# Broadcast comparisons and scalings on VectorE, rewritten column by column, in a kernel of four graph layers

## The reference

```python
# layer L0, messages both ways along each edge
mi  = concat([x[src_bi], x[tgt_bi], ef_bi])
h   = relu(layernorm(mi @ msg_w1 + msg_b1)) @ msg_w2 + msg_b2
agg = segment_sum(h, tgt_bi)
# layer L1, softmax over the edges that leave a node
p   = exp(e - segment_max(e, src)[src])
p   = p / segment_sum(p, src)[src]
agg = segment_sum(normalize(feat)[src] * p[:, None], dst)
```

## Time and profile before

| | |
|---|---|
| median of 3 runs | 5807.9 us (5806.9 to 5809.72) |
| the profiled execution | 5813.95 us, its span 5812.2 us |
| VectorE busy | 4147.4 us (71%) |
| GpSimd busy | 4255.6 us (73%) |
| TensorE, ScalarE busy | 4197.8 us (72%), 3623.6 us (62%) |

### The profile page before, as it was taken

One profiled execution on the slowest core, in us unless ns is written; L12 is line 12 of the kernel. 1 busy time (PEld: TensorE's weight loads), 2 busy tenths in 40 slices (PEclk: granted clock), 3 DMA queues, 4 the chain that ended last, 5 costly groups with the idle time before them and its releaser, 6 DMA issues.

```text
span 5812.2 us, 83096 instructions
## 1 busy us (share of the span) xinstructions
PE 4197.8 (72%) x23224; PEld 3139.8 (54%) x23301; DVE 4147.4 (71%) x10603; ACT 3623.6 (62%) x12357; POOL 4255.6 (73%) x3819
## 2 busy tenths in 40 slices
PE   3766666666676666663688888568888884999995
PEld 2655565656565656663455555335555553555553
DVE  4867777777777676773688888657777775777775
ACT  3767666666667676762477777447767763555553
POOL 4788888888888888885477777577777753777776
PEclk6877777777777777776799999779999996999997
DMA  8776766666666767664366766456766662555553
GB/s 235 167 172 159 172 165 168 165 168 165 167 170 162 173 158 173 163 155 92 100 194 195 196 195 194 131 177 210 214 210 211 209 187 59 151 160 158 160 158 105
DMA packets 629375, 976.98 MB, mean 168 GB/s; under 512 B 105432, under 2 KB 339026, under 8 KB 628642
## 3 DMA queue, kind: packets, MB, share of 16 engines
q1 hardware_dynamic: 394242, 616.15, 33.6%
q0 software_dynamic: 234656, 355.35, 29.4%
HBM read 668.41 MB, written 306.11 MB: 168 GB/s over the span
## 4 chain that ended last, share of the span: by engine, by line
POOL 58%; issue 20%; PE 7%; DMA 6%; DVE 4%; ACT 2%; SPq 2%; POOLq 1%; DVEq 0%; ACTq 0%
POOL arena L1515 30%; POOL tab L1160 16%; POOL arena L1179 11%; DMA tab<-arena 3%; DMA arena<-T,srcI 2%; PE PS L1978 1%; POOLq L1173 1%; PE PS L1678 1%; POOL arena L1212 1%; PE PS L301 1%; PE PS L1956 1%; PE PS L1473 1%; ACT arena L1269 0%; SPq L786 0%; PE PS L1359 0%
## 5 line engine op out<-in xcount | busy, mean ns | idle before, releaser
L1515 POOL DMA_INDIRECT arena<-T,srcI x2112 | 2033.0, 963 | 843.9 <-issue 631.4
L1160 POOL DMA_INDIRECT tab<-arena x784 | 1286.9, 1641 | 279.4 <-issue 228.7
L1179 POOL DMA_INDIRECT arena<-T,srcI x784 | 802.4, 1023 | 286.5 <-issue 283.8
L1502 DVE TENSOR_TENSOR_SCAN arena<-arena,PS 128x512 f32<-128x512 bf16 x588 | 748.6, 1273 | 181.0 <-PE PS L2256 81.5
L851 PE MATMUL PS<-arena 128*128 128x128 f32 x1568 | 308.5, 358 | 674.3 <-ACT arena L1107 674.3
L1482 ACT ACTIVATE arena<-PS 128x512 f32<-128x512 f32 x588 | 347.3, 591 | 646.0 <-PE PS L1473 646.0
L1582 DVE TENSOR_SCALAR arena<-PS,nodeid 128x512 bf16<-128x512 f32 x908 | 627.6, 739 | 75.4 <-PE PS L1563 75.4
L851 PEld LDWEIGHTS PS<-arena 128*128 128x128 f32 x1568 | 265.5, 256 | 713.5 <-ACT arena L1107 713.5
L932 DVE CUSTOM_DVE_ANT_0 arena<-arena,ltri 128x128 f32<-128x128 f32 x784 | 224.7, 287 | 499.2 <-ACT arena L1083 499.2
L832 PE MATMUL PS<-We,arena 65*128 65x256 f32 x1568 | 513.9, 411 | 86.3 <-DVE arena L874 60.5
L2238 PE MATMUL PS<-arena 128*128 128x512 bf16 x2323 | 546.5, 382 | 4.4 <-issue 0.4
(11 more groups left out here) (287 smaller groups left out, 10294.5 us busy)
## 6 DMA issues: line engine op xcount, KB each, us to landing
H<-arena SPq DMA_DIRECT2D x784, 256.0 KB, 2.3
arena<-keepR SPq DMA_DIRECT2D x294, 256.0 KB, 5.2
arena<-sF SPq DMA_DIRECT2D x98, 512.0 KB, 5.8
arena<-wF SPq DMA_DIRECT2D x98, 512.0 KB, 7.2
arena<-dF SPq DMA_DIRECT2D x98, 512.0 KB, 8.6
arena<-T,srcI POOLq DMA_INDIRECT x2896, 3.8
arena<-in_ea64T SPq DMA_DIRECT2D x98, 256.0 KB
arena<-S SPq DMA_DIRECT2D x98, 256.0 KB
```

What stands on the lines that cost most here:

```text
L1160: e.indirect_dma_start(out=tabs[k % KT], out_offset=at_rows(iA[b % 10][:, c:c + 1]), in_=X2[b % 3][:, c, :], in_offset=None, compute_op=AL ...
L1179: e.indirect_dma_start(out=Gs[b % NR][:, c, :], out_offset=None, in_=T0, in_offset=at_rows(srcI[:, CB * b + c:CB * b + c + 1])).then_inc(g ...
L1502: ins = e.tensor_tensor_scan(s[b % n][:, h, :], kR[g % 6][:, h0:h0 + CB * P], src[h], s[(b - 1) % n][:, h, CB * P - 1:CB * P] if b else in ...
L1515: e.indirect_dma_start(out=dst[:, c, :], out_offset=None, in_=T_tab, in_offset=at_rows(srcI[:, CB * b + c:CB * b + c + 1])).then_inc(gs.of ...
```

## The change

Each tensor_tensor with a broadcast column becomes a row of tensor_scalars, one to a column, whose scalar is a [128, 1] operand, so each has one streamed input in place of two. `OH` is gone: `RH` is now made in 16 instructions of 25 elements, each a comparison and a multiplication by two [128, 1] operands; for that the mask `fst` is first multiplied by `mg` and by `sg` (two instructions of 8 elements, into the new `first`).

```diff
             def dve_S1(e, b):
...
-                e.tensor_tensor(Sm[b % 6], sR[g % 3][:, h0:h0 + CB * P].rearrange("p (c f) -> p c f", f=P),
-                                bf(srcF[:, CB * b:CB * b + CB]), ALU.is_equal).then_inc(S1.of(0), 1)
+                for c in range(CB):
+                    k = CB * b + c
+                    ins = e.tensor_scalar(Sm[b % 6][:, c, :], sR[g % 3][:, h0 + c * P:h0 + (c + 1) * P], srcF[:, k:k + 1],
+                                          None, ALU.is_equal)
+                ins.then_inc(S1.of(0), 1)
...
             def dve_D(e, b):
...
-                t = Gs[b % NR].rearrange("p c (h f) -> p (c h) f", h=2)[:, 0:C2 - ND, :]
-                e.tensor_tensor(t, t, bf(rst[g % 3][:, o:o + C2 - ND]), ALU.mult).then_inc(D.of(0), 1)
+                t = Gs[b % NR].rearrange("p c (h f) -> p (c h) f", h=2)
+                for k in range(C2 - ND):
+                    ins = e.tensor_scalar(t[:, k, :], t[:, k, :], rst[g % 3][:, o + k:o + k + 1], None, ALU.mult)
+                ins.then_inc(D.of(0), 1)
 
             def dve_A(e, b):
                 g = b // 2
-                sl = slice(C2 * g, C2 * g + C2)
-                e.tensor_tensor(OL, bc(iotaf[:, :], C2), bf(loF[:, sl]), ALU.is_equal)
-                e.tensor_tensor(OH, bc(iotaf[:, 0:NBLK], C2), bf(hiF[:, sl], NBLK), ALU.is_equal)
                 e.tensor_scalar(fst, cb[g % 4], 0.5, None, ALU.is_lt).then_inc(A1.of(0), 1)
+                for c in range(C2):
+                    k = C2 * g + c
+                    e.tensor_scalar(OL[:, c, :], iotaf[:, :], loF[:, k:k + 1], None, ALU.is_equal)
                 e.wait_ge(A1.of(0), A1.at(2 * g))
-                e.tensor_tensor(OH, OH, bf(fst, NBLK), ALU.mult).then_inc(A1.of(0), 1)
+                e.wait_ge(ex.of(0), ex.at(b))
+                e.tensor_tensor(first[:, 0, :], fst, mg[g % 4], ALU.mult)
+                e.tensor_tensor(first[:, 1, :], fst, sg[g % 4], ALU.mult).then_inc(A1.of(0), 1)
                 e.wait_ge(A1.of(0), A1.at(2 * g + 1))
-                e.wait_ge(ex.of(0), ex.at(b))
-                e.tensor_tensor(RH[:, :, 0, :], OH, bf(mg[g % 4], NBLK), ALU.mult)
-                e.tensor_tensor(RH[:, :, 1, :], OH, bf(sg[g % 4], NBLK), ALU.mult).then_inc(RHd.of(0), 1)
+                for c in range(C2):
+                    k = C2 * g + c
+                    for n in range(2):
+                        ins = e.tensor_scalar(RH[:, c, n, :], iotaf[:, 0:NBLK], hiF[:, k:k + 1], first[:, n, c:c + 1],
+                                              ALU.is_equal, ALU.mult)
+                ins.then_inc(RHd.of(0), 1)
...
             def dve_scale(e, b):
...
-                e.tensor_tensor(g_[:, :, 0:P], g_[:, :, 0:P], bf(pp[b % 4]), ALU.mult).then_inc(D.of(0), 1)
+                for c in range(CB):
+                    ins = e.tensor_scalar(g_[:, c, 0:P], g_[:, c, 0:P], pp[b % 4][:, c:c + 1], None, ALU.mult)
+                ins.then_inc(D.of(0), 1)
```

More of the change, by code:

```diff
@@ L713, in L0_edges @@
             OL = arena.get(C2, P)
-            OH = arena.get(C2, NBLK)
-            fst = arena.get(C2)
+            fst, first = arena.get(C2), arena.get(2, C2)
             RH = arena.get(C2, 2, NBLK)
```

## The result

| | before | after |
|---|---|---|
| median of 6 runs | 5808.11 us (5805.64 to 5819.26) | 5780.06 us (5774.73 to 5789.72) |
| the profiled execution | 5813.95, span 5812.2 us | 5779.78, span 5777.7 us |

The ratio is 0.9951, with a 95% interval from 0.9938 to 0.9964: 28 us or 0.5% faster, where 67 were forecast. The time lies in the range; less than half of the gain came.

A forecast was written before the change was run, and what follows sets the result against it. Each edge stage was taken to last as long as GpSimd's chain of indirect DMAs. First stage -60, second -12, filling +5: -67 us, from 5807.9 to 5741 us; the forecast's own range was 5690 to 5795, the whole range 5690 to 5820.

The forecast's parts named there:

- VectorE idles 636/88 = 7.2 us per group, so this costs nothing there: First stage: VectorE's added time, 270 us over the stage, lies under its idle time and costs nothing.
- rival 4: Gain eaten by starts locked to VectorE's pattern or GpSimd, earlier, waiting for landed scatters; about 5800 us, chance 0.11.
- +2.7 us a group: First stage: VectorE's added time per group of two batches, taking 0.20 us per 128-element tensor_scalar and 0.145 per 25-element one.
- the rate of `dve_OT`: From 512 elements in 0.40 us: tensor_scalars stream about twice as fast as two-input instructions, plus 0.13 us fixed.
- The formula: An instruction holding for L per period T delays a GpSimd DMA by L²/2T in the mean, if starts fall anywhere.
- GpSimd idle only by issue: Sign of being right: GpSimd's only idle time is the 0.30 us between its instructions.
- Filling: At the start, while GpSimd waits 28.6 us for the first result, VectorE's added time counts: +5 us.
- high end: Range's slow case: each new instruction holds GpSimd for 0.286 us, half squares 1.45 in place of 0.71, -10 us in all.
- Rival 1: GpSimd does not get in between neighbouring VectorE instructions, so whole runs hold it; 6163 us, slower, chance 0.12.
- a gap between any two neighbours: GpSimd's DMA, if held, gets in between two neighbouring VectorE instructions, even when another two-input one follows at once.
- Rival 2: VectorE becomes the bound, at 0.286 us for each new instruction; about 5950 us, slower, chance 0.06.
- Rival 3: Double-rate tensor_scalars stop GpSimd's writing too, for the whole instruction; about 6470 us, slower, chance 0.05.

The follow-up runs named there:

- Before_slow_dve: The kernel before with four unused reductions of 784 elements added on VectorE at the end of `dve_A`; ratio 1.0093 to the kernel before.
- before_late: The kernel before with one wait added, so SyncE's row loads go out only after the third scatter of batch i-11 has landed; ratio 1.0125 to the kernel before.
- after_early: The changed kernel with SyncE's row loads issued one iteration sooner, ahead of the store, behind a wait for a landed scatter; ratio 0.9954 to the kernel before.
- after_kt4: The changed kernel with four tables for the scatters in place of three; ratio 0.9938 to the kernel before.
- no_rh: The changed kernel without the 16 instructions of 25 elements, `OH` and `RH` made as in the kernel before; ratio 0.9963 to the kernel before.
- sets A and B: Two of three sets of follow-up runs (A on one chip, B and C on another); the kernel before takes 6366 us (A), 6321 (B), 6379 (C).
- after_again: The changed kernel run once more, unaltered, in set B; ratio 1.0029 to the kernel before.
- before_again: The kernel before run once more, unaltered, in set C; ratio 1.0001 to the kernel before.
- tt_split: As no_rh, but each piece of 128 elements is a tensor_tensor with two inputs in place of a tensor_scalar; ratio 1.0101 to the kernel before.

## Why the prediction was right or wrong

**The step that failed** is "VectorE idles 636/88 = 7.2 us per group, so this costs nothing there". VectorE's time was indeed covered for VectorE: it still waits 240.7 us for ScalarE. But its prefix sum is what TensorE, ScalarE, the store and, behind the store in the same queue, the loads follow. They move against the scatters, and the landings pay. Before_slow_dve shows the whole chain and before_late its second link alone; after_early, after_kt4 and no_rh show the cure. The prediction weighed the end of this chain, as rival 4 ("GpSimd, earlier, waits for landed scatters"), with a chance of 0.11 and 8.1 us of wait in view. It gave the wrong cause (GpSimd's pace), and the sum held no term for it. The term is +45.7 us of idle time at the scatters (279.4 to 325.1), over the whole stage, against -57 of durations.

**The size of VectorE's cost.** +2.7 us a group became 3.6. The 25-element instructions caused it: 0.205 us, not 0.145, and 16 x 0.060 = 0.96 us. A piece of 25 elements costs what one of 128 does, which the rate of `dve_OT` could not show; the row nearest to it, line 1289, had 128 elements. In sets A and B this part is the whole difference between no_rh (faster) and after_again (slower).

**Right:** the lengths of the DMAs. The formula said -60 us for the first stage and the trace has -57; -12 for the second stage, and it is -17 in this pair; scatters 1.597 us and gathers 0.999 and 0.960 for 1.59 to 1.60, 0.99 and 0.965. The new tensor_scalars of 128 elements are 0.200 to 0.209 us apart, for 0.20, and VectorE waits 2.7 us a group for ScalarE, for 3. **Not right:** "GpSimd idle only by issue". Filling is not settled: the first scatter is 3.3 us earlier in this pair, for 5 later, and 2.3 later in after_again than in before_again.

**Luck in the -57.** The formula takes starts to fall anywhere, and they do not. Over the stage the new instructions held GpSimd for 27.4 us, where the formula has 0.71/26.2 x 1568 = 42. `dve_OT` and the short instruction right ahead of it (lines 982 and 976) held it for 27.0 us, 82 and 24 starts; in the kernel before that was 1.7 us, 10 and 6 starts, and the formula has 10 both times. A gather at 1490.59 us, which starts beside `dve_OT` and takes 1.16 us, is one of these. The two errors nearly cancel. This is the locking of starts to VectorE's pattern, the other half of rival 4; the lengths above contain it.

**A slip in the range.** Its high end takes 1.45 for 42 instructions that hold 0.286 us each; 42 x 0.286²/2 is 1.72, no gain at all in the first stage. That would have moved the forecast's high end up by some 16 us.

**Rival 1** (runs hold like one instruction) fails for tensor_scalars: none of 540 starts is held for more than 0.26 us. It holds for one run of two-input pieces, `OL` of tt_split, and fails for `dve_S1` there. My reading of the earlier trace rows as a gap between any two neighbours was too wide; the earlier trace rows showed the other case. **Rival 2** didn't occur: VectorE has 317 us of idle time left. **Rival 3:** the gather at 1489.26 us lies beside five tensor_scalars of 128 elements and takes 1.02 us, 0.08 over the floor; those at 668 us take 0.95. By the Trainium skill (SBUF — State Buffer, section "Who interferes with whom") a two-port tensor_scalar shuts GpSimd out for its whole length, which would have given DMAs that grow where a run lies inside them. The trace does not agree, if these instructions ran in such a mode, which no run shows: those 540 starts were held 0.05 us in the mean.

**Open:** why the second to fourth stages last longer in sets A to C, with waits of GpSimd on TensorE and on "remote" (TensorE's granted clock from 2900 to 3600 us is 0.94 of full speed, 2.4 GHz, in the pair's before and 0.87 in before_again, and which of the two follows from the other is not shown); why a landing takes longer behind the loads; what makes the `OL` run hold GpSimd; and the second stage's gain, seen in one pair of traces alone.

## What to carry to other kernels

An engine that has idle time is covered only against its own end. Before a cost on it is put at zero, follow what its instructions trigger, through every queue, to the transfers that share time with the ones that bound the kernel; here 3.6 us a group on VectorE moved three loads of 512 KB onto the landing of a scatter. Beside indirect DMAs a wide two-input instruction is worth cutting into tensor_scalars; small two-input pieces can hold a DMA for their whole run, as `OL` did here. And no piece should be so small that its fixed cost rules. A buffer more (a fourth table) tells a true gain from one that a wait has eaten.

## What the runs showed of the hardware

- A tensor_scalar with a [128, 1] operand takes 0.196 us (128 fp32 elements) or 0.202 us (25 elements) from start to start in a run of its kind, medians of the kernel after; a tensor_tensor of 128 elements also 0.202 (tt_split).
- A run of eight two-input instructions of 128 elements that all read `iotaf` held a gather that started 0.10 us into it until its own end and that of the two-input instruction behind it (2.79 us), and 78 of 81 starts in this way; runs of four and five such instructions on other tiles did not. Runs of tensor_scalars held none of 540 starts for more than 0.26 us.
- A scatter that starts 5 to 6 us after the issue of the `sF` load (the first of three of 512 KB) lands 5.1 us after its end in the mean, at 7 to 8 us 3.8, at 9 to 10 us 2.5, at 11 to 13 us 1.8 (worked out from the trace of the kernel after).
- The same kernel took 5808 us in one set of runs and 6321 to 6379 in three others, with an equal first stage and a second one 15% longer; on one chip two sets were 6321 and 6379.
